# Between two attentions: the inner normalisation moved from VectorE to ScalarE, its bias terms to GpSimd, and the transposes of the next group placed between a group's keys and its values

## The chip, the cores and the metric

The program runs on one core of a Trainium2 chip. The metric is the device time in microseconds (us) of one execution. The kernel before took 5235.08 us, the median of three runs (5229.41 to 5239.11). Engine names below: PE is TensorE (matmuls and transposes), DVE is VectorE, ACT is ScalarE, POOL is GpSimd, SP is SyncE, which here issues the transfers.

## The reference, cut to what matters

The reference is four layers on x of shape (4, 2048, 256), each of the form x = x + layernorm(layer(layernorm(x))): an RWKV attention, a mixture of experts, a rotary attention with 16 heads, and a "sliced" attention with 8 heads. The stage of this case ends the third layer and begins the fourth:

```
x  = x + _layernorm(attention_1_output)          # "outer" norm, eps 1e-5, no weights
y  = _layernorm(x)                               # the norm in front of layer 4
for e in range(4):                               # slices of 512 tokens of each of 4 batches
    xn = ((y_e - mean) * rsqrt(var + eps)) * norm_w + norm_b     # the "inner" norm of the slice
    m  = 256 // 2 ** e                           # only the first m features are used
    q, k, v = (xn[:, :m] @ w[:, :m].T + b for each of q, k, v)
```

Both norms in front of the projections act on the same row of 256 features, so the kernel does them in one step: it takes mean and variance of x once, and one scale per token that stands for the two divisions. norm_w is multiplied into the weights, norm_b and the projection biases are gathered into the biases of the results.

## The kernel before, in words

The program is a chain of phases. This case touches only `phase_sliced`, between the two attentions (names `r_...` in the trace, `r6_...` in the listings of instruction order). It handles 8192 tokens in 16 groups g of 512 tokens (4 tiles j of 128). Group g is slice e = g % 4 of its batch, and its matmuls read 256, 128, 64 or 32 features for e = 0, 1, 2, 3 (two chunks c for e = 0, one otherwise). A matmul in fp32 is recorded twice in the trace, so a group with e = 0 has 16 records for queries and keys and 16 for values, the others 6 and 8.

Each engine works through its own list in program order and waits on semaphores. For one group:

- SP loads A (the attention's output, 3 buffers) and X (the residual, 3 buffers); it later stores XS (the shifted x), the high and low parts of q and k (HI, LO) and the values (VB).
- DVE: `stats_a(g)` takes mean and variance of A (L1554, L1558); POOL `scale0(g)` makes 1/sqrt(var+eps), RS0 (L1447, L1449); DVE `add(g)` forms X = A*RS0 + X (L1567) and NB0 = -mean*RS0 (L1571); `stats_x(g)` takes mean and variance of X (L1577, L1581); POOL `scale1(g)` makes `scales` (L1453, L1455, L1457); DVE `inner(g)` writes XI = (X - mean)*scale (L1589).
- ACT: `shifted(g)` writes XS = X + NB0 (L1524).
- PE: `turn(g)` transposes XI into PSUM, tile PT (L1486); ACT `copy_turned(g)` copies PT to XT (L1531); PE `project(g)` makes q and k in PO (L1502) and v in PV (L1508).
- ACT `high(g)` rounds PO with its bias to HI (L1540); DVE `low(g)` makes the rest, LO (L1599); DVE `values(g)` takes PV to VB (L1607) when the value matmuls of g are done.

The loops set the order. PE: turn(g), queries and keys of g, values of g. ACT: shifted(g), copy_turned(g), high(g). DVE, per turn of its loop: add(g), stats_x(g), stats_a(g+1), inner(g), low(g-1), values(g-1). POOL: scale1(g), scale0(g+1). SP: load(g+2), store(g), store_qkv(g-1). XI, XT, HI, LO, VB and XS have two buffers each, PT and PV one.

Of the kernel before, what the change touches and what calls it, by code (L numbers as in the profile page):

```python
# [7 lines left out]
ALU = mybir.AluOpType  # L8
# [3 lines left out]
P = 128  # L12
# [3 lines left out]
J = GT // P  # L16
# [1316 lines left out]
def phase_sliced(nc, ao_d, x_d, xnew_d, scales, ident_d, w_d, bias_d, nw_d, nb_d, qk_d, v_d):  # L1333
# [6 lines left out]
    with ExitStack() as ctx:  # L1340
# [8 lines left out]
        VE1 = m.sb("VE1", [P, 2, J])  # L1349
        NB0 = [m.sb(f"NB0{u}", [P, J]) for u in range(2)]  # L1350
        nhalf = m.sb("nhalf", [P, 2, J])
# [15 lines left out]
            "const_ld", "half_set", "stat0", "stat1", "var0", "var1", "eps0", "eps1", "rs0", "rs1"))  # L1367
        nb0_done, x_sum, xs_done, xi_done, turned, xt, proj, vproj = (m.sem(n) for n in (
            "nb0_done", "x_sum", "xs_done", "xi_done", "turned", "xt", "proj", "vproj"))
        hi_done, lo_done, v_done, nb_wide, w_scaled, b_put, b_done = (m.sem(n) for n in (  # L1370
# [69 lines left out]
        @block.gpsimd  # L1440
        def _(pool):
            nc.gpsimd.memset(nhalf[:, :, :], -0.5).then_inc(half_set, 1)
            pool.wait_ge(half_set, 1)

            def scale0(g):
                wait(pool, var0, g + 1)
                nc.gpsimd.tensor_scalar(VE0[:, :], MV0[:, :, 1], EPS, None, ALU.add).then_inc(eps0, 1)  # L1447
                wait(pool, eps0, g + 1)
                nc.gpsimd.tensor_tensor(RS0[:, :], VE0[:, :], nhalf[:, 0, :], ALU.pow).then_inc(rs0, 1)  # L1449

            def scale1(g):
                wait(pool, var1, g + 1)
                nc.gpsimd.tensor_scalar(VE1[:, 0, :], MV1[:, :, 1], 1.0 + EPS, EPS * EPS, ALU.mult,  # L1453
                                        ALU.add).then_inc(eps1, 1)
                nc.gpsimd.tensor_scalar(VE1[:, 1, :], MV1[:, :, 1], EPS, None, ALU.add).then_inc(eps1, 1)  # L1455
                wait(pool, eps1, 2 * g + 2)
                nc.gpsimd.tensor_tensor(scales[:, g, :, :], VE1[:, :, :], nhalf[:, :, :], ALU.pow).then_inc(rs1, 1)  # L1457

            scale0(0)
            for g in range(NGR):  # L1460
                scale1(g)
                if g + 1 < NGR:
                    scale0(g + 1)

        @block.tensor
        def _(pe):
# [22 lines left out]

            def project(g):  # L1490
                e, u = g % E4, g % 2
# [5 lines left out]
                for a in range(2):  # L1497
                    wait(pe, lo_done, so_far(g - 1, CC * a + (CC if a else len(rows((g - 1) % E4))) - 1))
                    for h in range(CC if a else len(ks)):
                        for c, k in enumerate(ks):  # L1500
                            lo = a * D + h * P
                            ins = nc.tensor.matmul(PO[a][:, h, :], WS[0:k, c, lo:lo + P], XT[u][0:k, c, :],  # L1502
                                                   start=(c == 0), stop=(c == len(ks) - 1))
                    ins.then_inc(proj, 1)
                wait(pe, v_done, g)
                for j in range(J):
# [3 lines left out]
                ins.then_inc(vproj, 1)  # L1510

            for g in range(NGR):
                turn(g)
                project(g)

        @block.scalar
        def _(act):
            def shifted(g):
# [4 lines left out]
                for j in range(J):  # L1523
                    ins = nc.scalar.activation(XS[u][:, j, :], X[g % NX][:, j, :], ACT.Identity,  # L1524
                                               bias=NB0[u][:, j:j + 1])
                ins.then_inc(xs_done, 1)

            def copy_turned(g):
# [13 lines left out]

            act.wait_ge(const_ld, 16 * 6)
            for g in range(NGR):
                shifted(g)
                copy_turned(g)
                high(g)

        @block.vector
        def _(dve):  # L1550
# [10 lines left out]
            def add(g):  # L1561
# [3 lines left out]
                for j in range(J):  # L1565
# [3 lines left out]
                ins.then_inc(x_sum, 1)  # L1569
                wait(dve, xs_done, g - 1)  # L1570
                nc.vector.scalar_tensor_tensor(out=NB0[g % 2][:, :], in0=MV0[:, :, 0], scalar=-1.0, in1=RS0[:, :],  # L1571
                                               op0=ALU.mult, op1=ALU.mult).then_inc(nb0_done, 1)

            def stats_x(g):
                wait(dve, x_sum, g + 1)
                for j in range(J):
                    ins = nc.vector.bn_stats(ST1[:, j, :], X[g % NX][:, j, :])  # L1577
                ins.then_inc(stat1, 1)
                wait(dve, stat1, g + 1)
                for j in range(J):  # L1580
                    ins = nc.vector.bn_aggr(MV1[:, j, :], ST1[:, j, :])  # L1581
                ins.then_inc(var1, 1)

            def inner(g):
                u = g % 2
                wait(dve, rs1, g + 1)
                wait(dve, turned, g - 1)
                for j in range(J):
                    ins = nc.vector.tensor_scalar(XI[u][:, j, :], X[g % NX][:, j, :], MV1[:, j, 0:1],  # L1589
                                                  scales[:, g, 0, j:j + 1], ALU.subtract, ALU.mult)  # L1590
                ins.then_inc(xi_done, 1)

# [23 lines left out]
            for g in range(NGR):  # L1616
                add(g)
                stats_x(g)
                if g + 1 < NGR:
                    stats_a(g + 1)  # L1620
                inner(g)
                if g == 0:
# [834 lines left out]
```

## Time and profile before

| | |
|---|---|
| median of three runs | 5235.08 us |
| the profiled execution: time, span | 5222.77 us, 5220.7 us |
| busy share of the span: PE, DVE, ACT, POOL | 91%, 81%, 66%, 26% |
| the stage, from its first transposes to its last value matmul | 4009.14 to 4201.30 us |

The profile is one execution. Its page gives busy time by engine over the whole program, which is governed by the two attentions; for this change only the stage counts, so it is read by stretches. Times in the rows below are us from the start of the span. In a timeline, a row is a run of like instructions: start, length from the first's start to the last's end, engine, line, operation, result and operands, count, and in brackets how long the engine had been idle and what ended that. "PEclk" in a table of stretches is the granted TensorE clock as a share of 2.4 GHz: 0.50 is 1.2 GHz, 1.00 is 2.4 GHz.

### The profile page before, as it was taken

The page shows a single profiled execution, that of the slowest core. Times are in us where ns is not written, and L with a number is a line of the kernel's source. Part 1 is how long each engine was busy: PE and PEld are TensorE (multiplying, and loading weights), DVE is VectorE, ACT ScalarE, POOL GpSimd, SP SyncE. Part 2 cuts the span into 40 slices and gives each one's busy share as a digit, 9 for nine tenths or more (in the row PEclk, how much of TensorE's full clock was granted, in tenths as well). Part 3 has the DMA queues.
Part 4 walks back from the last instruction along what each step waited for, and adds up shares of the span by engine and source line. Part 5 has one row for each costly group of instructions (what it writes and reads, how often), then busy time and mean ns, then how long its engine had stood idle before and what let it go on. Part 6 is the DMA issues. An engine that isn't in the chain of part 4 may idle for free. (4 is left out here: it accounts for less than half of the span.)

```text
span 5220.7 us, 99043 instructions
## 1 busy us (share of the span) xinstructions
PE 4729.6 (91%) x34043; PEld 2092.8 (40%) x34043; DVE 4233.1 (81%) x5517; ACT 3452.1 (66%) x6176; POOL 1334.8 (26%) x881
## 2 busy tenths in 40 slices
PE   6999674697899999999999999999998879999983
PEld 3444451364333333333333333333334435455532
DVE  6999651297999999989999999999993877777726
ACT  4777210032588888888888888888885326666663
POOL 2323220065000000000000000000001229999991
PEclk9999896898799999999999999999998659999996
DMA  5110469788333333333333333333313931323204
GB/s 182 49 53 37 162 215 349 265 275 242 51 56 54 47 48 48 55 50 54 48 48 48 48 53 55 51 47 48 52 30 97 305 107 42 82 58 80 68 7 162
DMA packets 345777, 499.12 MB, mean 96 GB/s; under 512 B 67137, under 2 KB 254305, under 8 KB 328257
## 3 DMA queue, kind: packets, MB, share of 16 engines
q1 hardware_dynamic: 323776, 467.47, 37.5%
q10 hardware_dynamic: 21504, 25.17, 1.3%
q8 instruction: 295, 4.83, 0.4%
q14 instruction: 202, 1.65, 0.1%
HBM read 325.15 MB, written 165.02 MB: 94 GB/s over the span
## 5 line engine op out<-in xcount | busy, mean ns | idle before, releaser
L771 DVE TENSOR_REDUCE at_NM<-at_MX 128x1 f32<-128x1024 f32 (+1 forms) x3008 | 3082.0, 1050 | 326.3 <-PE at_MX L603 294.4
L713 ACT ACTIVATE at_PB<-at_S 128x512 f32<-128x512 f32 x5056 | 2720.0, 597 | 602.2 <-PE at_S L632 499.9
L603 PE MATMUL at_MX<-at_KT,at_QT 48*128 48x512 f32 (+1 forms) x5056 | 1920.8, 455 | 75.1 <-DMA at_VS<-v 54.3
L632 PE MATMUL at_S<-at_QT,at_KT 50*128 50x512 f32 (+1 forms) x5056 | 1903.6, 442 | 5.4 <-ACT at_PB L713 5.2
L644 PE MATMUL at_AV<-at_PB,at_VS 128*32 128x256 f32 (+1 forms) x18304 | 1574.0, 415 | 15.8 <-ACT at_AVS L721 13.2
L632 PEld LDWEIGHTS at_S<-at_QT,at_KT 50*128 50x128 f32 (+1 forms) x5056 | 802.1, 187 | 880.8 <-issue 480.8
L603 PEld LDWEIGHTS at_MX<-at_KT,at_QT 48*128 48x128 f32 (+1 forms) x5056 | 791.2, 190 | 328.0 <-DVE at_NM L771 215.3
L644 PEld LDWEIGHTS at_AV<-at_PB,at_VS 128*32 128x32 f32 x18304 | 364.3, 108 | 862.6 <-ACT at_PB L713 746.6
L537 POOL CAST at_NMR<-at_NMF 16x128 fp32r<-16x128 f32 x79 | 22.1, 280 | 1634.0 <-ACT at_NMF L726 1634.0
L564 POOL TENSOR_TENSOR at_SUM<-at_SUM,at_PB 128x2048 f32<-128x2048 f32 x90 | 415.6, 4618 | 11.5 <-ACT at_PB L713 0.9
L911 PE MATMUL wkv_PQ<-wkv_XT,wkv_WT 128*128 128x512 f32 x768 | 340.6, 600 | 42.9 <-DVE wkv_DL L1031 25.4
L564 POOL TENSOR_TENSOR at_SUM<-at_PB 128x2048 f32<-128x2048 f32 x75 | 352.4, 4702 | 29.0 <-ACT at_PB L713 27.9
L547 POOL TENSOR_TENSOR at_O<-at_FO,at_REC 128x256 f32<-128x256 f32 x64 | 39.8, 621 | 1023.3 <-DVE at_REC L782 1023.3
L911 PEld LDWEIGHTS wkv_PQ<-wkv_XT,wkv_WT 128*128 128x128 f32 x768 | 144.6, 191 | 238.3 <-issue 194.2
L990 POOL TENSOR_TENSOR wkv_EV<-wkv_E2S,wkv_V 128x1024 f32<-128x1024 f32 x32 | 75.6, 2361 | 356.5 <-DVE wkv_MN L1009 153.1
L924 PE MATMUL wkv_NP<-wkv_T,wkv_ident 128*128 128x512 f32 x256 | 118.7, 607 | 16.7 <-DVE wkv_T L1046 16.7
L1213 PE MATMUL r_PA<-r_OC,r_A 128*128 128x256 f32 x512 | 115.4, 385 | 13.6 <-DMA r_A<-ycat 13.6
L1817 PE MATMUL r_QK<-r_WC,r_XT 128*128 128x512 f32 x256 | 120.2, 593 | 0.6 <-DVE r_WC L1976 0.6
L1502 PE MATMUL r_PO<-r_XT,r_WS 128*128 128x512 f32 (+2 forms) x136 | 93.6, 851 | 17.8 <-ACT r_XT L1531 17.8
L1213 PEld LDWEIGHTS r_PA<-r_OC,r_A 128*128 128x128 f32 x512 | 97.8, 193 | 27.5 <-DVE r_OC L1322 14.4
L726 ACT ACTIVATE at_NMF<-at_S 16x128 f32<-16x128 f32 x79 | 21.0, 266 | 131.1 <-PE at_S L623 131.1
L2292 PE MATMUL fin_PA<-fin_OW,fin_AT 128*128 128x256 f32 (+3 forms) x160 | 41.3, 423 | 70.6 <-DMA fin_AT<-ao 68.8
(209 smaller groups left out, 3514.3 us busy)
## 6 DMA issues: line engine op xcount, KB each, us to landing
moe_W<-in_w SPq DMA_DIRECT2D x64, 1024.0 KB, 11.9
at_QT<-qk SPq DMA_DIRECT2D x408, 128.0 KB, 5.2
at_KT<-qk SPq DMA_DIRECT2D x384, 128.0 KB, 6.8
qk<-r_HI SPq DMA_DIRECT2D x52, 512.0 KB, 4.9
qk<-r_LO SPq DMA_DIRECT2D x52, 512.0 KB, 5.4
at_VS<-v SPq DMA_DIRECT2D x96, 256.0 KB, 9.0
at_KT<-qk SPq DMA_DIRECT2D x96, 256.0 KB, 6.3
ycat<-wkv_Y SPq DMA_DIRECT2D x32, 512.0 KB, 2.6
```

The costliest lines, as they stand in the source:

```text
L564: nc.gpsimd.tensor_tensor(total[:, :, :], other, PB[:, k:k + NCH, :], ALU.add).then_inc(sum_done, 1)
L603: ins = nc.tensor.matmul(MX[r][:, a, :], q_of(s)[h:h + NQ, b * P:(b + 1) * P], k_of(it, s, b * P // W)[h:h + NQ, (c + a) * W:(c + a + 1) * W],
L632: nc.tensor.matmul(SP_[item(it, s, "score", t)[1]][:, :], k_of(it, s, c)[h:h + NQ + 2, kb * P:(kb + 1) * P], q_of(s)[h:h + NQ + 2, c * W:( ...
L644: ins = nc.tensor.matmul(AV[c * VW:(c + 1) * VW, cols], v_of(it, s, c)[:, kb, :], PB[:, (NCH * kb + c) % NPB, cols], start=first, stop=last)
L713: nc.scalar.activation(PB[:, t % NPB, :], SP_[r][:, :], ACT.Exp, scale=scale).then_inc(exp_done, 1)
L771: nc.vector.tensor_reduce(NM4[:, b, c:c + 1], MX[r][:, :, :].rearrange("p a n -> p (a n)"), AX_X, ALU.max, negate=True).then_inc(ring_got, 1)
L911: ins = nc.tensor.matmul(PQ[q][:, tt * 512:(tt + 1) * 512], WT[:, cc, row:row + P], XT[b % 2][:, cc, t0:t0 + 512], start=(cc == 0), stop=( ...
L924: ins = nc.tensor.matmul(NP[:, t], ident[:, :], part[s][:, t], start=(k == 0), stop=(k == 1))
L990: nc.gpsimd.tensor_tensor(EV[s][:, :], E2S[s][:, :], V[s][:, :], ALU.mult).then_inc(pv, 1)
L1213: ins = nc.tensor.matmul(PA[u][:, j, :], A[u][:, q, j * P:(j + 1) * P], OC[:, q, :], start=(q == 0), stop=(q == NC - 1))
L1502: ins = nc.tensor.matmul(PO[a][:, h, :], WS[0:k, c, lo:lo + P], XT[u][0:k, c, :], start=(c == 0), stop=(c == len(ks) - 1))
L1817: ins = nc.tensor.matmul(QK[j % 2][:, :], XT[u][:, c, j * P:(j + 1) * P], WC[:, c, 0:2 * D], start=(c == 0), stop=(c == CC - 1))
```

## The change

Three edits, all in `phase_sliced`. `inner(g)` leaves DVE and becomes four ACT activations, XI = scale*X + NB1, so its scale and its bias are both per-token operands. POOL makes the negative means NM0 and NM1 and the products NB0 and NB1 with the scales. PE and ACT loops are written in another order: turn(g+1) stands between the keys and the values of g, ACT does inner(g+1) between copy_turned(g) and high(g), and shifted(g+1) after high(g). The order of what is left on DVE, and SP's list, are as they were.

```diff
@@ gpsimd
             def scale0(g):
                 wait(pool, var0, g + 1)
                 nc.gpsimd.tensor_scalar(VE0[:, :], MV0[:, :, 1], EPS, None, ALU.add).then_inc(eps0, 1)
-                wait(pool, eps0, g + 1)
+                nc.gpsimd.tensor_scalar(NM0[:, :], MV0[:, :, 0], -1.0, None, ALU.mult).then_inc(eps0, 1)
+                wait(pool, eps0, 2 * g + 2)
                 nc.gpsimd.tensor_tensor(RS0[:, :], VE0[:, :], nhalf[:, 0, :], ALU.pow).then_inc(rs0, 1)
+                wait(pool, xs_done, g - 1)
+                wait(pool, rs0, g + 1)
+                nc.gpsimd.tensor_tensor(NB0[g % 2][:, :], NM0[:, :], RS0[:, :], ALU.mult).then_inc(nb0_done, 1)
 
             def scale1(g):
...
-                wait(pool, eps1, 2 * g + 2)
+                nc.gpsimd.tensor_scalar(NM1[:, :], MV1[:, :, 0], -1.0, None, ALU.mult).then_inc(eps1, 1)
+                wait(pool, eps1, 3 * g + 3)
                 nc.gpsimd.tensor_tensor(scales[:, g, :, :], VE1[:, :, :], nhalf[:, :, :], ALU.pow).then_inc(rs1, 1)
+                wait(pool, xi_done, g - 1)
+                wait(pool, rs1, g + 1)
+                nc.gpsimd.tensor_tensor(NB1[g % 2][:, :], NM1[:, :], scales[:, g, 0, :], ALU.mult).then_inc(nb1_done, 1)
@@ tensor
+            turn(0)
             for g in range(NGR):
-                turn(g)
-                project(g)
+                project_qk(g)
+                if g + 1 < NGR:
+                    turn(g + 1)
+                project_v(g)
@@ scalar
+            def inner(g):
+                u = g % 2
+                wait(act, nb1_done, g + 1)
+                wait(act, turned, g - 1)
+                for j in range(J):
+                    ins = nc.scalar.activation(XI[u][:, j, :], X[g % NX][:, j, :], ACT.Identity,
+                                               bias=NB1[u][:, j:j + 1], scale=scales[:, g, 0, j:j + 1])
+                ins.then_inc(xi_done, 1)
...
+            inner(0)
+            shifted(0)
             for g in range(NGR):
-                shifted(g)
                 copy_turned(g)
+                if g + 1 < NGR:
+                    inner(g + 1)
                 high(g)
+                if g + 1 < NGR:
+                    shifted(g + 1)
@@ vector
-                wait(dve, xs_done, g - 1)
-                nc.vector.scalar_tensor_tensor(out=NB0[g % 2][:, :], in0=MV0[:, :, 0], scalar=-1.0, in1=RS0[:, :],
-                                               op0=ALU.mult, op1=ALU.mult).then_inc(nb0_done, 1)
...
                 wait(dve, x_sum, g + 1)
+                wait(dve, eps1, 3 * g)
...
-            def inner(g):
-                u = g % 2
-                wait(dve, rs1, g + 1)
-                wait(dve, turned, g - 1)
-                for j in range(J):
-                    ins = nc.vector.tensor_scalar(XI[u][:, j, :], X[g % NX][:, j, :], MV1[:, j, 0:1],
-                                                  scales[:, g, 0, j:j + 1], ALU.subtract, ALU.mult)
-                ins.then_inc(xi_done, 1)
...
-                inner(g)
```

What PE executes, from the transposes of one group to the values of the next (two groups with e = 2 and 3; PO0 holds queries, PO1 keys, PV values; PT is the transposed tile). Before:

```order
L1486 MATMUL r6_PT<-r6_ident,r6_XI0 128x128 x8
L1502 MATMUL r6_PO0<-r6_XT0,r6_WS 128x512
L1502 MATMUL r6_PO1<-r6_XT0,r6_WS 128x512 x2
L1508 MATMUL r6_PV<-r6_WS,r6_XT0 128x256 x4
L1486 MATMUL r6_PT<-r6_ident,r6_XI1 128x128 x8
L1502 MATMUL r6_PO0<-r6_XT1,r6_WS 128x512
L1502 MATMUL r6_PO1<-r6_XT1,r6_WS 128x512 x2
L1508 MATMUL r6_PV<-r6_WS,r6_XT1 128x256 x4
```

The same place of the changed kernel:

```order
L1511 MATMUL r6_PO0<-r6_XT0,r6_WS 128x512
L1511 MATMUL r6_PO1<-r6_XT0,r6_WS 128x512 x2
L1495 MATMUL r6_PT<-r6_ident,r6_XI1 128x128 x8
L1520 MATMUL r6_PV<-r6_WS,r6_XT0 128x256 x4
L1511 MATMUL r6_PO0<-r6_XT1,r6_WS 128x512
L1511 MATMUL r6_PO1<-r6_XT1,r6_WS 128x512 x2
L1495 MATMUL r6_PT<-r6_ident,r6_XI0 128x128 x8
L1520 MATMUL r6_PV<-r6_WS,r6_XT1 128x256 x4
```

The values of a group (PV from XT0) now stand behind the transposes of the group after it (PT from XI1).

What DVE executes in one turn of its loop, between two groups' values. Before:

```order
L1607 TENSOR_TENSOR r6_VB1<-r6_PV,r6_BVE 128x1024
L1567 SCALAR_TENSOR_TENSOR r6_X0<-r6_A0,r6_RS0,r6_X0 128x256 x4
L1571 SCALAR_TENSOR_TENSOR r6_NB01<-r6_MV0,r6_RS0 128x4
L1577 BN_STATS r6_ST1<-r6_X0 128x6 x4
L1581 BN_AGGR r6_MV1<-r6_ST1 128x2 x4
L1554 BN_STATS r6_ST0<-r6_A1 128x6 x4
L1558 BN_AGGR r6_MV0<-r6_ST0 128x2 x4
L1589 TENSOR_SCALAR r6_XI1<-r6_X0,r6_MV1,scales 128x256 x4
L1599 SCALAR_TENSOR_TENSOR r6_LO0<-r6_PO0,r6_BCE,r6_HI0 128x512
L1599 SCALAR_TENSOR_TENSOR r6_LO0<-r6_PO1,r6_BCE,r6_HI0 128x512 x2
L1607 TENSOR_TENSOR r6_VB0<-r6_PV,r6_BVE 128x1024
```

The same place of the changed kernel:

```order
L1625 TENSOR_TENSOR r6_VB1<-r6_PV,r6_BVE 128x1024
L1596 SCALAR_TENSOR_TENSOR r6_X0<-r6_A0,r6_RS0,r6_X0 128x256 x4
L1604 BN_STATS r6_ST1<-r6_X0 128x6 x4
L1608 BN_AGGR r6_MV1<-r6_ST1 128x2 x4
L1583 BN_STATS r6_ST0<-r6_A1 128x6 x4
L1587 BN_AGGR r6_MV0<-r6_ST0 128x2 x4
L1617 SCALAR_TENSOR_TENSOR r6_LO0<-r6_PO0,r6_BCE,r6_HI0 128x512
L1617 SCALAR_TENSOR_TENSOR r6_LO0<-r6_PO1,r6_BCE,r6_HI0 128x512 x2
L1625 TENSOR_TENSOR r6_VB0<-r6_PV,r6_BVE 128x1024
```

XI and NB0 are gone from the list; the sum into X0 still stands right behind VB1, the values of two groups earlier.

What ACT executes in one turn of its loop of the changed kernel (XT is the copy of the transposed tile, XI the normalised rows of the next group, HI the high parts, XS the shifted x):

```order
L1555 ACTIVATE r6_XT1<-r6_PT 128x1024
L1548 ACTIVATE r6_XI0<-r6_X0,r6_NB10,scales 128x256 x4
L1564 ACTIVATE r6_HI1<-r6_PO0,r6_BCE 128x512
L1564 ACTIVATE r6_HI1<-r6_PO1,r6_BCE 128x512 x2
L1539 ACTIVATE r6_XS0<-r6_X0,r6_NB00 128x256 x4
```

Before, a turn was XS, XT, HI of one group, with no XI.

## Rows read from the trace of the kernel before

**Rows 1.** Table of stretches: engines' busy us (and instructions), clock, DMA.
```profile
core 0: us, PE busy (x) PEld busy (x) DVE busy (x) ACT busy (x) POOL busy (x), PEclk, DMA share, GB/s
4060.20:4108.20 48.00, 41.61 (x106) 23.63 (x106) 39.25 (x118) 18.80 (x33) 13.84 (x20) 0.68 1.01 306
```

**Rows 2.** Waits from 4011.9 to 4201.4: total us, times, longest.
```profile
PE r_PO L1502 <- ACT r_XT L1531: 17.8, 16, 1.1
...
PE r_PT L1486 <- DVE r_XI L1589: 7.8, 4, 2.0
```

**Rows 3.** Timeline, PE, from the keys of e = 3 through a whole batch.
```profile
4048.34 5.48 PE L1502 MATMUL r_PO<-r_XT,r_WS 32*128 32x512 f32 x6 [1.11 <-ACT r_XT L1531]
...
4053.62 3.62 PE L1508 MATMUL r_PV<-r_WS,r_XT 32*128 32x256 f32 x8
...
4057.17 1.97 PE L1486 MATMUL r_PT<-r_ident,r_XI 128*128 128x128 f32 x8
...
4060.25 9.64 PE L1502 MATMUL r_PO<-r_XT,r_WS 128*128 128x512 f32 x16 [1.11 <-ACT r_XT L1531]
...
4069.73 3.62 PE L1508 MATMUL r_PV<-r_WS,r_XT 128*128 128x256 f32 x16
...
4073.19 1.04 PE L1486 MATMUL r_PT<-r_ident,r_XI 128*128 128x128 f32 x8
...
4078.02 1.89 PE L1508 MATMUL r_PV<-r_WS,r_XT 128*128 128x256 f32 x8
...
4081.86 1.48 PE L1486 MATMUL r_PT<-r_ident,r_XI 128*128 128x128 f32 x8 [1.95 <-DVE r_XI L1589]
```

**Rows 4.** Timeline, DVE, POOL, ACT: from the values of one group to XI.
```profile
4055.02 1.70 ACT L1524 ACTIVATE r_XS<-r_X,r_NB 128x256 f32<-128x256 f32 x4
...
4057.28 1.23 DVE L1607 TENSOR_TENSOR r_VB<-r_PV,r_BVE 128x1024 f32<-128x1024 f32 x1 [0.81 <-PE r_PV L1508]
4058.42 1.67 DVE L1567 SCALAR_TENSOR_TENSOR r_X<-r_A,r_RS,r_X 128x256 f32<-128x256 f32 x4
...
4060.12 1.41 DVE L1577 BATCH_NORM_STATS2 r_ST<-r_X 128x6 f32<-128x256 f32 x4
...
4061.56 0.38 DVE L1581 BATCH_NORM_AGGREGATE r_MV<-r_ST 128x2 f32<-128x6 f32 x4
...
4062.03 0.19 POOL L1453 TENSOR_SCALAR r_VE<-r_MV 128x4 f32<-128x4 f32 x1 [7.50 <-DVE r_MV L1581]
...
4062.30 0.23 POOL L1455 TENSOR_SCALAR r_VE<-r_MV 128x4 f32<-128x4 f32 x1
...
4062.61 1.67 POOL L1457 TENSOR_TENSOR scales<-r_VE,r_nhalf 128x8 f32<-128x8 f32 x1
```

**Rows 5.** Groups by line: busy us, mean ns; ACT with and without bias, POOL.
```profile
L721 ACT ACTIVATE at_AVS<-at_AV 128x512 f32<-128x512 f32 x79 | 47.7, 603 | 8.0 <-PE at_AV L644 8.0
L1540 ACT ACTIVATE r_HI<-r_PO,r_BCE 128x512 fp32r<-128x512 f32 x52 | 33.5, 684 | 81.7 <-PE r_PO L1502 81.7
L1449 POOL TENSOR_TENSOR r_RS<-r_VE,r_nhalf 128x4 f32<-128x4 f32 x16 | 18.6, 1159 | 1.3
```

**Rows 6.** Timeline: the first group's sum, statistics, POOL and value matmuls.
```profile
4010.59 1.67 DVE L1567 SCALAR_TENSOR_TENSOR r_X<-r_A,r_RS,r_X 128x256 f32<-128x256 f32 x4
...
4014.20 0.19 POOL L1453 TENSOR_SCALAR r_VE<-r_MV 128x4 f32<-128x4 f32 x1 [10.58 <-DVE r_MV L1581]
...
4021.82 3.62 PE L1508 MATMUL r_PV<-r_WS,r_XT 128*128 128x256 f32 x16
```

**Rows 7.** Timeline, PE: the last group.
```profile
4192.40 5.48 PE L1502 MATMUL r_PO<-r_XT,r_WS 32*128 32x512 f32 x6 [1.11 <-ACT r_XT L1531]
4197.68 3.62 PE L1508 MATMUL r_PV<-r_WS,r_XT 32*128 32x256 f32 x8
```

**Rows 8.** Stretches of 5 us from e = 0 into e = 2.
```profile
4060.00:4065.00 5.00, 4.75 (x6) 2.17 (x7) 4.26 (x21) 0.20 (x1) 2.73 (x5) 0.50 1.01 340
4065.00:4070.00 5.00, 5.00 (x13) 2.16 (x13) 2.10 (x5) 1.33 (x3) 0.73 (x1) 0.97 1.10 318
...
4080.00:4085.00 5.00, 2.03 (x9) 1.58 (x10) 4.58 (x9) 2.09 (x4) 1.75 (x3) 0.74 1.03 254
```

More of the change, by code:

```diff
@@ L1349, in phase_sliced @@
         VE1 = m.sb("VE1", [P, 2, J])
-        NB0 = [m.sb(f"NB0{u}", [P, J]) for u in range(2)]
+        NB0, NB1 = ([m.sb(f"{q}{u}", [P, J]) for u in range(2)] for q in ("NB0", "NB1"))
+        NM0, NM1 = (m.sb(q, [P, J]) for q in ("NM0", "NM1"))
         nhalf = m.sb("nhalf", [P, 2, J])
@@ L1367, in phase_sliced @@
             "const_ld", "half_set", "stat0", "stat1", "var0", "var1", "eps0", "eps1", "rs0", "rs1"))
-        nb0_done, x_sum, xs_done, xi_done, turned, xt, proj, vproj = (m.sem(n) for n in (
-            "nb0_done", "x_sum", "xs_done", "xi_done", "turned", "xt", "proj", "vproj"))
+        nb0_done, nb1_done, x_sum, xs_done, xi_done, turned, xt, proj, vproj = (m.sem(n) for n in (
+            "nb0_done", "nb1_done", "x_sum", "xs_done", "xi_done", "turned", "xt", "proj", "vproj"))
         hi_done, lo_done, v_done, nb_wide, w_scaled, b_put, b_done = (m.sem(n) for n in (
@@ L1488, in turn, with project_qk @@
                 ins.then_inc(turned, 1)
-            def project(g):
+            def project_qk(g):
                 e, u = g % E4, g % 2
@@ L1504, in project, with project_v @@
                     ins.then_inc(proj, 1)
+            def project_v(g):
+                u, ks = g % 2, rows(g % E4)
                 wait(pe, v_done, g)
```

## The prediction, as put on record

> **What bounds the kernel now.** I first read the order of the stages and then the stretch that the change touches, 4009.14 to 4201.30 us of a span of 5220.7, so a stage of 192 us, 3.7% of the time. Nothing else in the program changes. The table of stretches comes first [rows 1]: one batch of four groups takes 48.00 us, in which PE is busy for 41.61, DVE for 39.25, ACT for 18.80 and POOL for 13.84, at a mean granted clock of 0.68. PE is the nearest to full, DVE close behind, and the transfers are near full too (share 1.01, 306 GB/s). Then the waits [rows 2]: in the 16 groups PE idles 17.8 us for the copy XT and, in four groups, 7.8 us for XI. That is 25.6 us, and it is what can at most be won on PE. The timeline of PE [rows 3] shows the chain of one group: transposes, 1.11 us of idle time, queries and keys, values, transposes of the next group at once. Last comes the timeline of the other engines [rows 4], since the change moves their work: what matters there is which instruction of DVE stands behind the value matmuls.
>
> **The circle that decides.** DVE takes its work in order, and its sum into X of group g+1 (add) stands right behind VB of group g-1 (values), which waits for the value matmuls V(g-1). So the rows of g+1 are never begun before V(g-1) has ended. Before, turn(g+1) comes on PE behind keys and values of g, so the way from V(g-1) to XI(g+1) lies beside turn(g), queries, keys and V(g), about two PE stretches; it costs only in the fast group, the 1.95 us of [rows 3] (7.8 us in all). After, V(g) stands behind turn(g+1), which waits for XI(g+1), which follows from V(g-1). Only queries and keys of g lie beside that way now; the transposes and the values are added to it. The period of a group is then: V(g-1) ends, values, add, stats_x, scale1, inner(g+1), turn(g+1), V(g) ends.
>
> I set V(g-1)'s end at zero and add up from the rows. Values start 0.04 later (4053.62 + 3.62 = 4057.24 in [rows 3], against 4057.28 in [rows 4]); to the sum's start 1.14; to bn_stats 1.70; to bn_aggr 1.44; to POOL's first instruction 0.47: together 4.79. From there to the pow 0.58, of which a third small instruction, NM1, adds one more step; the two there are have pitches of 0.27 and 0.31, I take 0.29: pow starts at 5.66. It takes 1.67 (7.33), then a gap of 0.08 as between L1455's end and the pow (all [rows 4]).
>
> The product NB1 is new on POOL: a 128x4 product of two tiles. The trace has none. From below it is the 0.19 of the shortest 128x4 instruction [rows 4], from above the 1.16 of a 128x4 pow [rows 5]; a product is nearer to the first, I take 0.25: NB1 at 7.66. A hop to ACT of 0.05 as the others: 7.71.
>
> Inner on ACT is new as well: 4 activations 128x256 with a scale and a bias per token. Four with a bias alone take 1.70 us [rows 4]. What an operand per token adds shows in 128x512: 684 ns with one against 603 without [rows 5], 81 ns. A second one adds between nothing and that, and I take all of it: 1.70 + 4 x 0.081 = 2.02. XI is ready at 9.73, turn(g+1) starts at 9.78. The Trainium skill, "ScalarE: Activation LUTs", section "What ACT_TABLE_LOAD costs", says that each operand read through a per-partition pointer adds about 93 ns to an ACTIVATE; the 81 ns of these rows agrees for the first, and no row here shows an activation with two. By its figure inner would be 2.07 us; by the rule left aside, 1.70 and the sum 4.5 us less.
>
> Then turn and V(g) to its end. At 1.2 GHz the transposes are 1.97 us [rows 3], of which some 0.20 overlaps what follows (5.48 against a pitch of 5.28 between keys and values), so 1.77, and V(g) 3.62: 5.39. With e = 0 at 2.4 GHz it is 1.04 - 0.16 = 0.88 and 3.62: 4.50. A period is 9.78 + 5.39 = 15.17 us for e = 1, 2, 3. For e = 0, queries and keys last 9.48 from their start to V's (4060.25 to 4069.73 [rows 3]), just under 9.78, so 9.78 + 4.50 = 14.28. A batch: 14.28 + 3 x 15.17 = 59.79 us instead of 48.00.
>
> **Which clock.** [Rows 8] show 0.50 when e = 0 begins, 0.97 in the second 5 us of it, and a fall to a mean of 0.74 in the 5 us in which PE had first waited 1.95 us for XI [rows 3]. After the change PE waits, in a group with e = 1, from the end of its short keys to 9.78, some 6 to 7 us, and 4.5 us in e = 2 and 3 (9.78 less 5.28). So I take 1.2 GHz from the transposes behind e = 1 on, up to the middle of the next e = 0, which is dense as before. The Trainium skill speaks against the change here: "TensorE: Matmul & The Clock Gate", section "HAM oscillation — how this bites in real kernels", says that where a wait separates bursts of matmuls, each burst can begin at the lower clock. The fall beside the 1.95 us wait agrees. By this rule a period with e = 1 is 15.17, without it 12.55.
>
> **Sum.** The first group: XI(1) is ready at 4014.20 + 0.58 + 0.29 + 1.67 + 0.08 + 0.25 + 0.05 + 2.02 + 0.05 = 4019.19 [rows 6], before queries and keys end (4021.82), so V(0) ends at 4021.82 + 4.50 = 4026.32. Groups 1 to 14 are 11 x 15.17 + 3 x 14.28 = 209.71. Group 15 has no turn behind it: 5.28 + 3.62 = 8.90 [rows 7]. V(15) ends at 4244.93; before it was 4197.68 + 3.62 = 4201.30. The stage grows by 43.6 us. What follows (values, stores, the next attention) keeps its length.
>
> **What costs nothing, and why.** The copy XT no longer stops PE: after XI (9.73) ACT has three HI at about 0.64 (11.65), XS 1.70 (13.35) and the copy 1.02 (14.4), before V(g) ends at 15.17; this is the gain of the 17.8 us, already inside the periods. In e = 0, with four HI, the copy comes some 0.8 us after V's end, and the keys behind it still end long before 9.78. Behind inner's wait on ACT stand HI(g), XS(g+1) and XT(g+1); LO(g) follows HI by 0.7 and is on DVE before VB(g), which waits for V(g) anyway. What DVE loses (1.38 us of inner, 0.16 of NB0, 0.67 waiting for the pow) stood behind the statistics, not on the way to them, so it shortens nothing in the circle. POOL's small instructions for NB0 come after the ones that DVE waits for. SP's waits on xi_done and xs_done come later by the clock of the longer group, with buffers three deep, and the transfers get more time, not less.
>
> **Rivals.** (1) Shorter stage: the circle does not bind, PE stays the bound, and all 25.6 us go: 5209. For it: DVE, ACT and POOL are all far from full by busy time [rows 1]. Against: busy shares don't see a circle of waits, and the order of DVE's list is in the code. Chance 0.04. (2) The same, but the transfers, at share 1.01, give PE nothing to win: 5235, within the bound. Chance 0.03. (3) The circle binds, but PE keeps 2.4 GHz from the first group on: a period of e >= 1 is then 9.78 + 0.88 + 1.89 = 12.55, the last group about 4.6; V(15) at 4211.8, +10.5 us: 5246. Against it stands the fall at the shorter wait. Chance 0.05. (4) The circle binds and PE never rises in e = 0: 16 records at 0.88 are 14.1, then 1.77 and 7.1, 23.0 in place of 14.3, four times: +78 us, 5313. Against: e = 0 begins behind a slow, dense stretch as before, where it rose within 5 us. Chance 0.04. My forecast has 0.84.
>
> **How the numbers follow.** The profiled execution took 5222.77 us, 2.07 more than its span and 12.3 less than the median of the three runs. With the sum it would be 5266.4; I add the same 43.6 to the median, 5235.08, and get 5279. Known ends: inner without the second operand's cost -4.5; XI's transposes and V(1) of each batch still at 2.4 GHz, 4 x 2.62 = -10.5; NB1 at 0.19 -0.8 and at 1.16 14 x 0.91 = +12.7; these give 5263 to 5291. The runs before differed by up to 6 us from their median. I widen a little to either rival: 5257 to 5294. A difference of more than 0.2%, 10.5 us, counts as one, about what a measurement can tell: faster 0.04 (rival 1), same 0.04 (rival 2 and a part of 3), slower 0.92.
>
> **What would show it.** Right: the batch of four groups takes about 60 us; PE's transposes wait for XI in nearly every group, 4 to 7 us at a time, some 60 us in all; its wait for XT is nearly gone; XI on ACT waits for NB1 of POOL; DVE's VB waits for the value matmuls in every group; the granted clock's mean in a batch is below 0.68. Four inner activations in 2.0 us and NB1 in about 0.25 us. Wrong: if XI is there when the keys end, or if the sum into X does not start about 1.1 us behind VB, the circle is misread; if PEclk stays at 1.00 through e = 1 and 2, rival 3.

## The result, and the profile after

The changed kernel takes 5275.23 us, the median of four runs (5271.15 to 5279.71), against 5232.44 for the kernel before (four runs, 5229.41 to 5239.11): ratio 1.0083, 95% interval 1.0063 to 1.0104, slower by 42.8 us. The forecast was +43.6, which it put at 5279 us with a range of 5257 to 5294. Of all the executions reported in this document one, of the experiment on the engine of inner, took 13436.87 us at a mean granted clock of 0.486; it is left out of that experiment's median.

In the profiled execution (time 5277.39 us, span 5275.2) the stage lasts from 4016.49 to 4254.65 us, 238.16 instead of 192.16, so +46.0. The span grew by 54.5: 7.35 of the rest lie ahead of the stage, in phases that are the same in both programs and differ from one execution to the next (in the thirteen profiles of this document the stage begins between 4009.11 and 4025.35 us). I therefore judge the stage by its own length.

The table of stretches of the kernel after answers to [rows 1]. The stretch has the forecast length of a batch, 59.80 us; from keys to keys of e = 0 the two middle batches took 59.56 and 60.49:

```profile
4071.80:4131.60 59.80, 39.96 (x106) 23.01 (x106) 33.97 (x97) 25.75 (x49) 17.07 (x37) 0.70 0.85 245
```

It holds 106 matmul records, as the 48.00 us of before did. PE is busy for 1.65 us less, while DVE lost 5.3 us a batch and the transfers fell to a share of 0.85 and 245 GB/s. No engine and no queue is near full: what sets the pace now is a chain, not a load. The waits of the kernel after over the stage, answering to [rows 2] (engine, tile, line, what was waited for, us in total, times, longest):

```profile
ACT r_XI L1548 <- POOL r_NB L1466: 125.9, 15, 9.5
PE r_PT L1495 <- ACT r_XI L1548: 71.9, 14, 7.3
DVE r_LO L1617 <- ACT r_HI L1564: 66.4, 17, 5.8
DVE r_VB L1625 <- PE r_PV L1520: 36.8, 15, 3.0
PE r_PO L1511 <- ACT r_XT L1555: 1.8, 4, 1.1
```

PE's wait for the copy XT went from 17.8 to 1.8 us, and the one for XI from 7.8 us in four groups to 71.9 in fourteen. The matmuls of the stage by shape, first before, then after (us busy, mean ns of one, idle time ahead), say where the 46.0 us are:

```profile
L1502 PE MATMUL r_PO<-r_XT,r_WS 128*128 128x512 f32 x88 | 49.7, 724 | 8.9 <-ACT r_XT L1531 8.9
L1486 PE MATMUL r_PT<-r_ident,r_XI 128*128 128x128 f32 x128 | 26.1, 370 | 7.8 <-DVE r_XI L1589 7.8
L1508 PE MATMUL r_PV<-r_WS,r_XT 128*128 128x256 f32 x96 | 22.0, 379 | 0.0
L1502 PE MATMUL r_PO<-r_XT,r_WS 32*128 32x512 f32 x24 | 21.9, 1083 | 4.5 <-ACT r_XT L1531 4.5
L1502 PE MATMUL r_PO<-r_XT,r_WS 64*128 64x512 f32 x24 | 21.9, 1084 | 4.5 <-ACT r_XT L1531 4.5
L1508 PE MATMUL r_PV<-r_WS,r_XT 64*128 64x256 f32 x32 | 14.5, 631 | 0.0
L1508 PE MATMUL r_PV<-r_WS,r_XT 32*128 32x256 f32 x32 | 14.5, 629 | 0.0
```

```profile
L1511 PE MATMUL r_PO<-r_XT,r_WS 128*128 128x512 f32 x88 | 48.5, 708 | 1.8 <-ACT r_XT L1555 1.8
L1495 PE MATMUL r_PT<-r_ident,r_XI 128*128 128x128 f32 x128 | 28.0, 391 | 71.9 <-ACT r_XI L1548 71.9
L1520 PE MATMUL r_PV<-r_WS,r_XT 128*128 128x256 f32 x96 | 27.6, 449 | 0.0
L1511 PE MATMUL r_PO<-r_XT,r_WS 32*128 32x512 f32 x24 | 21.9, 1083 | 0.0
L1520 PE MATMUL r_PV<-r_WS,r_XT 64*128 64x256 f32 x32 | 15.1, 652 | 0.0
L1520 PE MATMUL r_PV<-r_WS,r_XT 32*128 32x256 f32 x32 | 14.9, 645 | 0.0
L1511 PE MATMUL r_PO<-r_XT,r_WS 64*128 64x512 f32 x24 | 11.6, 617 | 0.0
```

Idle time rose from 25.7 to 73.7 us, +48.0, and busy time fell from 170.6 to 167.6, -3.0: together +45.0 of the 46.0 (neighbouring groups overlap by some tenths). So the loss is time in which PE waits for XI. The granted clock is a small gain on balance: keys of e = 2 ran at 2.4 GHz (11.6 us instead of 21.9), transposes (28.0 instead of 26.1) and the values that read 128 rows (27.6 instead of 22.0) more slowly.

One turn of the circle in the kernel after, from the end of a V to the end of the next; it answers to [rows 3] and [rows 4]:

```profile
4045.63 3.62 PE L1520 MATMUL r_PV<-r_WS,r_XT 128*128 128x256 f32 x8
4049.18 2.99 PE L1511 MATMUL r_PO<-r_XT,r_WS 64*128 64x512 f32 x6
4049.29 1.23 DVE L1625 TENSOR_TENSOR r_VB<-r_PV,r_BVE 128x1024 f32<-128x1024 f32 x1 [2.80 <-PE r_PV L1520]
4050.43 1.66 DVE L1596 SCALAR_TENSOR_TENSOR r_X<-r_A,r_RS,r_X 128x256 f32<-128x256 f32 x4
4052.13 1.41 DVE L1604 BATCH_NORM_STATS2 r_ST<-r_X 128x6 f32<-128x256 f32 x4
4053.57 0.38 DVE L1608 BATCH_NORM_AGGREGATE r_MV<-r_ST 128x2 f32<-128x6 f32 x4
4054.04 0.19 POOL L1458 TENSOR_SCALAR r_VE<-r_MV 128x4 f32<-128x4 f32 x1 [10.24 <-DVE r_MV L1608]
...
4054.93 1.67 POOL L1463 TENSOR_TENSOR scales<-r_VE,r_nhalf 128x8 f32<-128x8 f32 x1
4056.74 0.20 POOL L1466 TENSOR_TENSOR r_NB<-r_NM,scales 128x4 f32<-128x4 f32 x1
4056.98 2.07 ACT L1548 ACTIVATE r_XI<-r_X,r_NB,scales 128x256 f32<-128x256 f32 x4 [8.94 <-POOL r_NB L1466]
4059.10 1.97 PE L1495 MATMUL r_PT<-r_ident,r_XI 128*128 128x128 f32 x8 [6.93 <-ACT r_XI L1548]
4061.00 3.78 PE L1520 MATMUL r_PV<-r_WS,r_XT 64*128 64x256 f32 x8
```

V(g-1) ends at 4049.25, and the transposes start at 4059.10: 9.85 us, with each step the release of the next. The keys had been done since 4052.17.

### The profile page after: what moved, and what is told of

It is laid out like the page before. It is cut to its first block and busy times, and to the rows that moved or that the text cites. A ratio compares the mean times of both kernels' runs of the same rounds, so it can differ in the third digit from the quotient of the medians.

```text
span 5275.2 us, 99135 instructions
## 1 busy us (share of the span) xinstructions
PE 4738.8 (90%) x34043; PEld 2097.8 (40%) x34043; DVE 4211.9 (80%) x5437; ACT 3480.1 (66%) x6240; POOL 1346.8 (26%) x945
## 3 DMA queue, kind: packets, MB, share of 16 engines
q14 instruction: 201, 1.65, 0.1%
## 5 line engine op out<-in xcount | busy, mean ns | idle before, releaser
L1548 ACT ACTIVATE r_XI<-r_X,r_NB,scales 128x256 f32<-128x256 f32 x64 | 33.2, 589 | 147.4 <-POOL r_NB L1466 147.4
```

## Experiments

The stage length below is measured as above (192.2 before, 238.2 after), in the profiled execution of each. Ratios are against the kernel before, run on the same chip. "After" names the changed kernel. A period is the time from one group's end of V to the next group's. The texts put on record ahead of the runs number some of them: the first has the old position of the transposes, the fourth goes one group further ahead, the fifth has 16 more transposes, the tenth is the kernel before with one group further ahead.

**The position of the transposes alone.** After, with PE's loop in the old order. It takes turn(g+1) out of the way of V(g) and leaves all else.

```diff
-            turn(0)
             for g in range(NGR):
+                turn(g)
                 project_qk(g)
-                if g + 1 < NGR:
-                    turn(g + 1)
                 project_v(g)
```

> The changed kernel with PE's old order alone: transposes, queries and keys, values of each group; XI stays on ACT, NB0 and NB1 on POOL. Theory (the circle values, add, stats_x, scale1, XI, transposes, value matmuls of the group before): the transposes of g+1 are again behind keys and values of g, so the 9.8 us from V(g-1) to XI(g+1) lie beside about 10.7 us of PE work; a batch takes 48 to 49.5 us (before 48.0, after 59.8) and the time is 5232 to 5240. Rival (the cost sits in ACT's list, where XI holds up HI, LO and XT): nothing of that is undone, the time stays near 5270.

Measured: 5250.99 us, ratio 1.0028 (1.0015 to 1.0041), stage 205.2. The order of PE gives back 33.0 of the stage's 46.0 us; the time lies between the two that were expected, 5232 to 5240 and 5270, and is neither. Most of the rest is a second circle that I had not seen. DVE of this kernel in e = 2 and 3, with what ACT does between:

```profile
4102.64 1.21 DVE L1623 TENSOR_TENSOR r_VB<-r_PV,r_BVE 128x1024 f32<-128x1024 f32 x1
4103.77 1.66 DVE L1594 SCALAR_TENSOR_TENSOR r_X<-r_A,r_RS,r_X 128x256 f32<-128x256 f32 x4
...
4110.31 2.07 ACT L1546 ACTIVATE r_XI<-r_X,r_NB,scales 128x256 f32<-128x256 f32 x4 [6.11 <-POOL r_NB L1466]
4112.29 1.81 ACT L1562 ACTIVATE r_HI<-r_PO,r_BCE 128x512 fp32r<-128x512 f32 x3
4113.06 2.07 DVE L1615 SCALAR_TENSOR_TENSOR r_LO<-r_PO,r_BCE,r_HI 128x512 fp32r<-128x512 f32 x3 [4.07 <-ACT r_HI L1562]
4115.04 1.21 DVE L1623 TENSOR_TENSOR r_VB<-r_PV,r_BVE 128x1024 f32<-128x1024 f32 x1
```

VB, add, statistics, POOL, XI, HI, LO, VB: 12.40 us (4102.64 to 4115.04), with PE nowhere in it. On ACT, inner(g+1) stands ahead of HI(g), so HI waits for POOL; on DVE, low stands ahead of values and add, so DVE waits for HI.

**The order of ACT behind it.** The same kernel, with inner(g+1) behind high(g).

```diff
                 copy_turned(g)
-                if g + 1 < NGR:
-                    inner(g + 1)
                 high(g)
                 if g + 1 < NGR:
+                    inner(g + 1)
                     shifted(g + 1)
```

> PE's old order, as in the first experiment, and on ACT HI of g ahead of XI of g+1. The first experiment took 12.4 us a group in e = 2 and 3 with PE no longer in the circle. Theory: a second circle bound there, values, add, stats_x, scale1, XI, HI, LO, values, since XI stands ahead of HI on ACT and LO ahead of values on DVE; with HI ahead of XI it is open, PE sets the pace again, 48 to 49 us a batch, 5230 to 5238. If the cost is ACT's load itself (XI adds 2.07 us a group), it stays near 5246.

Measured: 5237.93 us, ratio 1.001 (0.9994 to 1.0025), stage 195.7, as expected. Of the 13.0 us that stayed after the old PE order, 9.5 were the place of one call in ACT's list. With both circles open, inner on ACT and the biases on POOL cost 3.5 us of stage and nothing that the times can tell.

**The engine of inner alone.** After, with `inner` on DVE again behind `stats_a`, without NM1 and NB1 on POOL; PE keeps the new order.

```diff
@@ gpsimd, scale1
-                nc.gpsimd.tensor_scalar(NM1[:, :], MV1[:, :, 0], -1.0, None, ALU.mult).then_inc(eps1, 1)
-                wait(pool, eps1, 3 * g + 3)
+                wait(pool, eps1, 2 * g + 2)
...
-                nc.gpsimd.tensor_tensor(NB1[g % 2][:, :], NM1[:, :], scales[:, g, 0, :], ALU.mult).then_inc(nb1_done, 1)
@@ scalar
-                if g + 1 < NGR:
-                    inner(g + 1)
@@ vector
+                for j in range(J):
+                    ins = nc.vector.tensor_scalar(XI[u][:, j, :], X[g % NX][:, j, :], MV1[:, j, 0:1],
+                                                  scales[:, g, 0, j:j + 1], ALU.subtract, ALU.mult)
...
                     stats_a(g + 1)
+                inner(g)
```

> The changed kernel with XI made by DVE again, as before the change (behind stats_a), NB1 gone; PE's new order and NB0 on POOL stay. Theory: the circle remains, only its way to XI is shorter, 8.7 us in place of 9.8, so a period is 14.0 to 14.3 in place of 15.2 to 15.5 and 14 periods give back 15 to 17 us: 5258 to 5261. Rival (XI in ACT's list is the cost): back to about 5232.

Measured: 5256.0 us (median of six), ratio 1.0046 (1.003 to 1.0062), stage 216.8. That is 2 us below the range expected, and the stage gave back 21.4 us where 15 to 17 were expected. PE in e = 2 and 3 of this kernel:

```profile
4049.51 1.97 PE L1491 MATMUL r_PT<-r_ident,r_XI 128*128 128x128 f32 x8 [5.74 <-DVE r_XI L1599]
...
4063.69 1.97 PE L1491 MATMUL r_PT<-r_ident,r_XI 128*128 128x128 f32 x8 [3.10 <-DVE r_XI L1599]
```

A period is 14.18 us in place of 15.53, as expected. With e = 1 the periods were 12.66 to 12.79 and not 14.0 to 14.3, since their values ran in 2.39 to 2.52 us, mostly at 2.4 GHz; that is the surplus. With the new PE order the move of inner and its biases puts 21.4 us on the stage; with both orders as in the experiment before, the moves put 3.5. A step's price depends on whether it stands in the circle.

**Opening the circle at DVE.** After, with values(g-2) behind stats_x(g), so that the sum into X no longer waits for V(g-1). Nothing else is changed: new PE order, inner on ACT, biases on POOL.

```diff
                 stats_x(g)
+                if g > 1:
+                    values(g - 2)
                 if g + 1 < NGR:
                     stats_a(g + 1)
@@
                     low(g - 1)
-                    values(g - 1)
+            values(NGR - 2)
             low(NGR - 1)
```

> The changed kernel with one move on DVE: values(g-1) stands behind add(g+1) and stats_x(g+1), no longer ahead of them. Theory: sum and statistics no longer wait for value matmuls; what is left is the way XI(g), HI and LO of g-1, add, statistics, POOL, XI(g+1), about 11.3 us, beside PE's 10.7: a batch takes 47 to 49 us, the time is 5230 to 5240. Rival (ACT's list): no effect, 5270 to 5275.

Measured: 5229.93 us, ratio 0.9991 (0.998 to 1.0002), stage 193.3. One call moved gives back 44.9 of the 46.0 us, and the time is the lower end of what was expected. A row from the table of stretches of this kernel, and the transposes of e = 3 in its timeline:

```profile
4072.10:4120.30 48.20, 40.08 (x107) 22.93 (x106) 33.66 (x98) 25.99 (x49) 16.89 (x36) 0.71 1.02 307
```

```profile
4103.48 1.97 PE L1495 MATMUL r_PT<-r_ident,r_XI 128*128 128x128 f32 x8 [3.97 <-ACT r_XI L1548]
```

The batch takes 48.20 us with nearly the same busy times as the 59.80 of after. PE still waits for XI (31.9 us in 11 groups), yet the next transposes start 11.28 us behind these (4114.76), where in after it was 15.53; the way expected to be left was about 11.3. This run shows the circle: it takes away no work and none of the moves, only the link from V(g-1) to the sum.

**Longer steps in the circle.** After, with four more small instructions (128x4, into tiles that nothing reads) between NM1 and the pow on POOL, an engine busy for 26% of the span.

```diff
-                wait(pool, eps1, 3 * g + 3)
+                wait(pool, eps1, 7 * g + 3)
+                for t in MORE:
+                    nc.gpsimd.tensor_scalar(t[:, :], MV1[:, :, 0], -1.0, None, ALU.mult).then_inc(eps1, 1)
+                wait(pool, eps1, 7 * g + 7)
...
-                wait(dve, eps1, 3 * g)
+                wait(dve, eps1, 7 * g)
```

> The changed kernel with four more 128x4 instructions on POOL (the negative mean written to four unused tiles) between NM1 and the pow: about 1.2 us of work in each group. Theory: they lie on the circle, each of 14 periods grows by 1.2 to 1.3 us, 16 to 18 us in all, about 5292. If POOL's way is not on the circle, no change from 5275.

Measured: 5295.04 us, ratio 1.0119 (1.0086 to 1.0151), stage 248.8. POOL of this kernel:

```profile
4081.67 0.78 POOL L1465 TENSOR_SCALAR r_MORE<-r_MV 128x4 f32<-128x4 f32 x4
4082.53 1.67 POOL L1467 TENSOR_TENSOR scales<-r_VE,r_nhalf 128x8 f32<-128x8 f32 x1
```

The four put the pow off by 0.86 us (4081.67 to 4082.53), not the 1.2 that I had worked out from the pitch of single ones. The first two small instructions and NM1 ahead of them start at 4080.77, 4081.05 and 4081.36, as far apart as in after. Fourteen periods times 0.86 are 12.0 us; the stage grew by 10.7, and e = 2's period went from 15.53 to 16.38. The hold-up passes into the stage almost whole, as a serial circle demands. The time is near the 5292 expected, but the interval of its ratio, 45 to 79 us above before, can't tell 12 us from 17; the stage can.

**What the clock costs.** Rival 3 had priced the slow transposes and values at up to 33 us. To hold the clock through the wait, 16 redundant transposes of XI[g] into PT (overwritten by the real ones) were put between keys and turn(g+1).

```diff
                 project_qk(g)
                 if g + 1 < NGR:
+                    for _ in range(2):
+                        for c in range(CC):
+                            for j in range(J):
+                                nc.tensor.transpose(PT[:, c, j * P:(j + 1) * P],
+                                                    XI[g % 2][:, j, c * P:(c + 1) * P], ident[:, :])
                     turn(g + 1)
```

> The changed kernel with 16 more transposes on PE in each group, between keys and the transposes of the next group: the rows of g are turned again into PT, where the next group's then overwrite them. They lie in the time in which PE waits for XI. If the lower clock is a part of what the circle costs, PE stays at 2.4 GHz through e = 1 to 3, transposes and values (5.4 to 5.7 us in the circle) shrink to about 2.8, and the time falls by 15 to 30 us to 5245 to 5260, although PE does more. If the clock plays no part, or stays low for narrow groups, 5270 to 5280.

Measured: 5290.12 us, ratio 1.0113 (1.0071 to 1.0154), stage 240.6. The time is above both ranges expected, and the run didn't test what it was for. PE of this kernel, from behind the keys of e = 1:

```profile
4100.03 1.91 PE L1531 MATMUL r_PT<-r_ident,r_XI 128*128 128x128 f32 x16
4107.47 1.97 PE L1495 MATMUL r_PT<-r_ident,r_XI 128*128 128x128 f32 x8 [5.53 <-ACT r_XI L1553]
```

The filler ran at 2.4 GHz and was over in 1.9 us; PE idled 5.53 us all the same, and the real transposes ran at 1.2 GHz. In e = 3 the filler itself ran at 1.2 GHz, in 3.67 us. So the same was done with 48 transposes (`range(6)`).

> As the fifth experiment, but 48 more transposes a group instead of 16. There the 16 ran at 2.4 GHz in 1.8 us where e = 1 and 2 wait 7 us, PE then idled for 5 us and the clock was low again for the transposes and values, so the question stayed open. 48 take 5.2 us at 2.4 GHz and leave PE 2 us idle. If the clock's fall is a part of the circle's cost, transposes and values of e = 1 to 3 now run at 2.4 GHz, periods fall from 15.4 to about 12.7 us and the time by 20 to 30 us, to 5245 to 5255. If it falls all the same, the 48 take up to 10.2 us where the clock is low, more than the wait of 4.4 us, and the time is above 5290.

Measured: 5281.02 us, ratio 1.0091 (1.0068 to 1.0113), stage 232.5; neither range expected holds the time. A stretch of this kernel, PE in one group with e = 1, and PE in e = 2 and 3:

```profile
4088.02:4148.00 59.98, 55.03 (x300) 42.20 (x301) 33.31 (x98) 26.01 (x49) 16.90 (x36) 0.91 0.86 253
```

```profile
4114.58 1.97 PE L1495 MATMUL r_PT<-r_ident,r_XI 128*128 128x128 f32 x8 [2.04 <-ACT r_XI L1553]
...
4182.37 7.33 PE L1531 MATMUL r_PT<-r_ident,r_XI 128*128 128x128 f32 x48
4189.54 1.04 PE L1495 MATMUL r_PT<-r_ident,r_XI 128*128 128x128 f32 x8
4190.50 1.99 PE L1520 MATMUL r_PV<-r_WS,r_XT 64*128 64x256 f32 x8
...
4195.19 5.46 PE L1531 MATMUL r_PT<-r_ident,r_XI 128*128 128x128 f32 x48
4202.36 1.09 PE L1495 MATMUL r_PT<-r_ident,r_XI 128*128 128x128 f32 x8 [1.71 <-ACT r_XI L1553]
```

With PE kept busy the granted clock is 0.91 over the batch, and in most groups transposes and values take 1.04 and 1.99 us. Where the filler ended before XI, the next transposes came 12.82 us behind the last ones (4189.54 to 4202.36), near the 12.55 of rival 3; six of the eleven periods with e = 1 to 3 were 12.68 to 12.88, in place of 14.11 to 15.53. So at 2.4 GHz a turn of the circle is shorter by some 2.7 us. But filler of 5.4 to 8.0 us often ended after XI, as at 4189.54, which shows no wait, and then it stands in the circle: those transposes had started 15.60 us behind the ones ahead of them. And in e = 0, where PE waits for at most 1.69 us in after, the periods grew: they were 14.40 to 14.70 us and became 16.63 to 19.61. The periods with e = 1 to 3 gave back 16.3 us together, those with e = 0 took 10.7: the stage shrank by 5.6 us, and the times show no gain over after. That PE's clock can be held through most waits is shown, and what it is worth in a turn; a gain in the time is not.

**One group further ahead.** After, with the sum and the statistics of g+1 done before DVE waits for anything of g, a fourth buffer for A and X, and loads three groups ahead.

```diff
-    NX = 3
+    NX = 4
@@ sync
+            load(2)
             for g in range(NGR):
-                if g + 2 < NGR:
-                    load(g + 2)
+                if g + 3 < NGR:
+                    load(g + 3)
@@ vector
-            for g in range(NGR):
+            def ahead(g):
                 add(g)
                 stats_x(g)
                 if g + 1 < NGR:
                     stats_a(g + 1)
+
+            ahead(0)
+            for g in range(NGR):
+                if g + 1 < NGR:
+                    ahead(g + 1)
```

> The changed kernel with add and stats_x taken one group further ahead on DVE (the sum of g+1 stands ahead of LO and values of g-1), with a fourth buffer of A and X and loads three groups ahead. Theory: the circle now spans two groups and does not bind; PE has neither the wait for XI nor that for XT and sets the pace, 10.7 us for e = 1 to 3 and 13.9 for e = 0 at the clock of before, 46 us a batch, less where the clock rises, until the transfers (share 1.01 at 48 us a batch) stop it at 44 to 45: 5215 to 5226, faster than both kernels. Rival (transfers leave nothing to win): 5230 to 5236.

Measured: 5214.16 us, ratio 0.9969 (0.9957 to 0.9982), stage 176.3, a little faster than expected. The same kernel once more:

> The kernel of the fourth experiment again, on one chip with the next. There it had a ratio of 0.9969 to the kernel before; expected 0.9955 to 0.9980.

Measured: 5210.8 us, ratio 0.996 (0.9945 to 0.9975), stage 174.0. It is faster than both kernels. How much of that is the order on DVE and how much the fourth buffer and the earlier loads was not taken apart. A batch and two of the waits of the first of these runs (the next batch took 46.50 us at share 1.03):

```profile
4058.80:4102.10 43.30, 40.36 (x107) 22.51 (x106) 32.61 (x96) 24.31 (x47) 15.87 (x35) 0.70 1.04 312
```

```profile
ACT r_HI L1565 <- DMA v<-r_VB: 41.3, 10, 6.7
...
DVE r_ST L1584 <- DMA r_A<-ao: 24.9, 9, 4.7
```

XI's wait for NB1 is all but gone on ACT (3.5 us against 125.9), and the longest waits now end with a store or a load. The last question is whether the change brings anything once the circle is open. So the same was done to the kernel before: `ahead`, four buffers, loads three ahead, `inner(g)` on DVE in front of `ahead(g + 1)`, old PE and ACT orders, NB0 on DVE as there.

> The kernel before with only what the fourth experiment added: add and stats_x one group further ahead on DVE, a fourth buffer of A and X; XI on DVE, PE's old order. PE still idles 1.11 us a group for XT (17.8 us in all) but no longer 7.8 us for XI: 5222 to 5228. That the fourth experiment is faster than this by about 10 us is what the change is worth once its circle is open; if this takes 5214 as well, the change's own parts are worth nothing.

Measured: 5224.45 us, ratio 0.9975 (0.9957 to 0.9993), stage 169.3; and once more:

> The kernel of the tenth experiment again (the kernel before with add and stats_x one group ahead), on one chip with the last. If the change's own parts (XI on ACT, transposes between keys and values) still win PE's 1.11 us a group once the circle is open, this is slower than the last by about 10 us. If the transfers set the pace in both (a share of 1.03 to 1.08 of the 16 engines in both profiles), the two agree within 5 us.

Measured: 5215.44 us, ratio 0.9973 (0.9963 to 0.9984), stage 173.1. A stretch of each second run, first the version of after, then that of before:

```profile
4060.00:4160.00 100.00, 91.62 (x234) 50.63 (x232) 73.91 (x216) 56.16 (x107) 36.82 (x80) 0.67 1.05 314
```

```profile
4060.00:4160.00 100.00, 83.82 (x244) 48.65 (x243) 83.87 (x255) 40.89 (x74) 30.18 (x45) 0.78 1.05 320
```

On the one chip the two agree within 5 us (4.6), as expected if the transfers set the pace. The intervals overlap in both pairs; by the ratios the version of after is faster by 3 and 7 us, which they can't tell from nothing, and its stage is the longer one both times. PE has 8 us in 100 more to spare in the version of before, DVE 10 in that of after, and it makes no difference that these runs can tell: the transfers stand at share 1.05 in both, at 314 and 320 GB/s. That they are the bound is read from that row and from the waits; no run took transfers away.

## Why the prediction was right

Every step of the sum for the circle can be held against the rows of after.

- **V(g-1)'s end to the transposes of g+1:** 9.78 predicted, 9.85 measured. NM1 put the pow off by 0.31 (0.29 taken), the gap behind the pow was 0.14 (0.08 taken), NB1 took 0.20 (0.25 taken), four inner activations 2.07 us (2.02 taken). The Trainium skill's price of an operand per token, "ScalarE: Activation LUTs", section "What ACT_TABLE_LOAD costs", gave 2.07 for inner, and the run agrees.
- **The periods:** 14.28 predicted for e = 0 and 14.40, 14.40 and 14.70 measured; 15.17 for the others and 15.53 measured in all seven groups with e = 2 and 3. Of the 0.36, 0.07 is the way just named and 0.29 a mis-sized term: I took V at 3.62 us, starting 1.77 behind the transposes' start. For values with 64 or 32 rows it starts 1.90 behind (4059.10 to 4061.00 in the circle above) and takes 3.78. With e = 1 the values read 128 rows, and the four periods were 15.22, 14.11, 15.04 and 15.23; in the second and third a part of the values still ran at 2.4 GHz (2.50 and 3.43 us). Over the groups 1 to 14 these are 7 x 0.36 = +2.5, +0.7 for e = 0 and -1.1 for e = 1, together +2.1: 211.8 us against 209.71.
- **First and last group:** V(0) ended 17.54 us behind the first transposes, 17.18 predicted, as queries and keys took longer; the last group took 8.83 instead of 8.90. Together that is the stage's +46.0 against +43.6. The times gave +42.8; their interval, 33 to 54 us (0.63% and 1.04% of 5232), holds both. That they came within 0.8 us of the sum is chance; the stage, which missed it by 2.4, is the better measure.
- **The copy XT and the cover of HI, LO and XS:** right. XT's wait is 1.8 us. In after, HI and LO were over before V ended: DVE waited for V another 36.8 us in fifteen groups.
- **What was off without touching the sum:** I expected a mean clock below 0.68 and some 60 us of waiting for XI. It was 0.70 and 71.9. I had taken 1.2 GHz from the transposes behind e = 1 on, but the keys of e = 2 ran at 2.4 GHz and ended earlier, so PE waited 6.9 to 7.1 us instead of 4.5 for the same moment. In the 5 us of the row below, of which PE was busy for 1.62 and then waited, the mean was still 0.94; the transposes at the end of the wait (4118.67) ran at 1.2 GHz:

```profile
4110.00:4115.00 5.00, 1.62 (x4) 0.37 (x2) 4.90 (x19) 0.00 (x0) 1.15 (x4) 0.94 1.04 361
```

- **What I did not see:** the circle over ACT's list. It was hidden in after, since 12.40 is less than 15.5, and came out when the first was opened. "Behind inner's wait on ACT stand HI(g), XS(g+1) and XT(g+1)" was noted, but the step from there back to DVE's add was not drawn.

Rivals 1 and 2, that PE or the transfers stay the bound, are refuted by the stretches with share 0.85 and by the run with values moved. Rival 3 did not occur in after: all transposes but those of e = 1 took 1.97 us; its period of 12.55 was nearly reached with filler (12.82). Rival 4 did not occur: PE reached 2.4 GHz in each e = 0 (queries and keys 8.52 to 10.13 us). One part stays open: why the experiment with 16 transposes, whose stage is only 2.4 us longer than after's, came out 15 us slower in the times, though the intervals of the two overlap.

## What to carry to other kernels

Before a step is moved in the list of an in-order engine, follow it once round: what it waits for, what stands ahead of that in the other engine's list, and so on until the chain meets the step again, and compare that sum with the period; busy shares (after: 40, 34, 26 and 17 of 60 us) don't show it. When such a circle binds, look for the link that is only an order and carries no data: here one call moved behind the statistics gave back 44.9 of 46.0 us, while the work moved between engines, with both circles open, was worth 3.5. Then look for the next circle just below it, and for the transfers, before counting on more.

## What the runs showed of the hardware that was not expected

- Eight value matmuls that read 64 or 32 rows took 3.78 us right behind transposes that read 128, against 3.62 behind keys of their own width, and started 0.14 us later behind the transposes than values that read 128.
- An activation 128x256 with a scale and a bias per token took 586 ns, one with a bias alone 501: 85 ns for the second operand, near the 81 that the first costs.
- On POOL, four like instructions on 128x4 took 0.78 us one behind another, 0.2 each, where single ones had a pitch of 0.27 to 0.31.
- A PE that waits 5.53 us after 1.9 us of filler at 2.4 GHz began again at 1.2 GHz; one that waited 1.71 us after 5.46 us of filler kept 2.4. Of four that waited 2.04 us after 5.40 us of filler, three kept 2.4 (transposes in 1.09 us) and one began at 1.2 (1.97 us): like waits did not always end alike.
